# Every second absolute weight sum of the V stage summed on ScalarE instead of VectorE

## The reference

```python
qkv = x @ w_qkv
q, k, v = jnp.split(qkv, 3, axis=-1)            # 16 heads of 64
q = _apply_rope(q, cos, sin); k = _apply_rope(k, cos, sin)
scores = jnp.einsum('bhqd,bhkd->bhqk', q, k) * scale
scores = jnp.where(causal, scores, jnp.finfo(scores.dtype).min)
out = jnp.einsum('bhqk,bhkd->bhqd', jax.nn.softmax(scores, axis=-1), v)
x = _layernorm(x + out @ w_out)

def _weight_quant(w):
    scale = 1.0 / jnp.clip(jnp.mean(jnp.abs(w)), 1e-05)
    return jnp.clip(jnp.round(w * scale), -1.0, 1.0) / scale
def _act_quant(x):
    scale = 127.0 / jnp.clip(jnp.max(jnp.abs(x), axis=-1, keepdims=True), 1e-05)
    return jnp.clip(jnp.round(x * scale), -128.0, 127.0) / scale

gate = silu(bitlinear(x, w_gate)); up = bitlinear(x, w_up)
x = _layernorm(x + bitlinear(gate * up, w_down))
```

## Time and profile before

| | before |
|---|---|
| median of 3 runs | 1207.52 us |
| the profiled execution's own time | 1206.47 us |
| its span, slowest core (core 0) | 1204.9 us |
| spans of the eight cores | 1201.3 to 1204.9 us |
| TensorE busy | 1143.7 us (95%) |
| VectorE busy | 703.1 us (58%) |
| ScalarE busy | 656.2 us (54%) |
| GpSimd busy | 115.3 us (10%) |

### The profile page before, as it was taken

One profiled execution on the slowest core, in us unless ns is written; L12 is line 12 of the kernel. 1 busy time (PEld: TensorE's weight loads), 2 busy tenths in 40 slices (PEclk: granted clock), 3 DMA queues, 4 the chain that ended last, 5 costly groups with the idle time before them and its releaser, 6 DMA issues.

```text
span 1204.9 us, 17116 instructions; the slowest of 8 cores (1201.3 to 1204.9 us)
## 1 busy us (share of the span) xinstructions
PE 1143.7 (95%) x6448; PEld 489.3 (41%) x6470; DVE 703.1 (58%) x999; ACT 656.2 (54%) x815; POOL 115.3 (10%) x185
## 2 busy tenths in 40 slices
PE   3998999999999988999999999999999999999998
PEld 1443333333333322444444444444444444444443
DVE  2359777677678634588874545545544544543343
ACT  3337699998999998354454344344344344342400
POOL 3011134122331230000000000000000000000000
PEclk9999899999999999999999999999999999999999
DMA  9999899976999784567784443443443433332482
GB/s 277 314 323 330 263 310 315 308 243 199 294 320 342 252 291 149 186 168 216 228 206 117 96 115 104 96 122 97 97 122 96 97 96 97 74 102 70 107 161 75
DMA packets 152705, 225.22 MB, mean 187 GB/s; under 512 B 107888, under 2 KB 112112, under 8 KB 137264
## 3 DMA queue, kind: packets, MB, share of 16 engines
q1 hardware_dynamic: 148784, 214.28, 60.7%
q0 software_dynamic: 3840, 9.84, 2.9%
HBM read 148.19 MB, written 46.53 MB: 162 GB/s over the span
## 4 chain that ended last, share of the span: by engine, by line
PE 75%; ACT 10%; DMA 8%; DVE 2%; POOL 2%; issue 1%; POOLq 0%; SPq 0%; DVEq 0%; ACTq 0%
PE sc L868 37%; PE av L932 16%; ACT E L644 7%; PE pj L401 6%; PE pj L787 5%; PE sc L631 4%; DMA ring<-wg 4%; PE av L671 3%; PE su L671 3%; PE sc L932 2%; DMA ring<-xu 2%; POOL swp L74 1%; DMA ring<-wu 1%; ACT Rb L693 1%; DMA swp<-QK 1%; DVE part L497 1%
## 5 line engine op out<-in xcount | busy, mean ns | idle before, releaser
L644 ACT ACTIVATE E<-sc,cst 128x1024 bf16<-128x1024 f32 (+1 forms) x288 | 292.2, 1069 | 32.5 <-PE sc L631 31.6
L878 ACT ACTIVATE sg<-sc,st 128x512 bf16<-128x512 f32 x128 | 87.7, 685 | 305.9 <-PE sc L868 280.5
L868 PE MATMUL sc<-TU,xqT 128*128 128x512 fp8e4 x1024 | 242.0, 379 | 0.0
L868 PE MATMUL sc<-TG,xqT 128*128 128x512 fp8e4 x1024 | 242.0, 379 | 0.0
L932 PE MATMUL av<-TD,hqT 128*128 128x512 fp8e4 x896 | 195.7, 379 | 0.0
L884 DVE TENSOR_TENSOR h<-sc,sg 128x512 f32<-128x512 f32 x128 | 88.2, 689 | 160.2 <-PE sc L868 137.9
L401 PE MATMUL pj<-xT,wqk 128*64 128x512 bf16 (+1 forms) x928 | 142.3, 395 | 19.8 <-DVE xT L354 18.8
L868 PEld LDWEIGHTS sc<-TG,xqT 128*128 128x128 bf16 x1024 | 100.2, 98 | 120.8
L868 PEld LDWEIGHTS sc<-TU,xqT 128*128 128x128 bf16 x1024 | 100.2, 98 | 120.9
L932 PEld LDWEIGHTS av<-TD,hqT 128*128 128x128 bf16 x896 | 87.6, 98 | 105.8
L631 PE MATMUL sc<-QK,QK 64*128 64x512 bf16 (+3 forms) x640 | 110.0, 355 | 21.1 <-ACT E L644 15.0
(11 more groups left out here) (88 smaller groups left out, 921.3 us busy)
## 6 DMA issues: line engine op xcount, KB each, us to landing
ring<-wg SPq DMA_DIRECT2D x28, 1024.0 KB, 19.3
ring<-wu SPq DMA_DIRECT2D x28, 1024.0 KB, 11.4
ring<-wd SPq DMA_DIRECT2D x16, 1024.0 KB, 11.0
dstg<-wd SPq DMA_DIRECT2D x16, 1024.0 KB, 7.0
hqs<-hq SPq DMA_DIRECT2D x64, 256.0 KB, 3.2
ring<-wqk SPq DMA_DIRECT2D x8, 1024.0 KB, 12.6
ring<-xu SPq DMA_DIRECT2D x8, 1024.0 KB, 25.1
swp<-QK POOLq DMA_DIRECT2D x64, 128.0 KB, 8.7
```

Of the source, the lines that this page charges most:

```text
L644: t2 = act.do(lambda e: e.activation(Et[:, :, a:z], out[:, :, a:z], AF.Exp, bias=c_(4), scale=0.125), t, *more)
L868: fn = lambda e, kc=kc, dst=dst, W=W: e.matmul(dst, x_[:, kc, :], W[:, n, kc * 512:(kc + 1) * 512], start=(kc == 0), stop=(kc == 7))
L878: a = act.do(lambda e: e.activation(sg[b], G[b], AF.Silu, scale=col(t, 19)), tm, t_hs[t], sg_free[b])
```

## The change

Of the units that fall into the V stage, every second call of `bg_item` asks for ScalarE, if the unit is an absolute sum and its number is below 12. The calls are counted with the weight conversion as number 1, so units 1, 3, 5, 7, 9 and 11 of the gate weight go to ScalarE and 0, 2, 4, 6, 8, 10 and 12 to 14 stay. ScalarE writes the absolute values over the unit in the ring and adds them up into the column of `part`.

```diff
+        t_parta = []
@@ bg_item
-        def bg_item():
+        def bg_item(on_act=False):
...
-                t = dve.do(lambda e: e.tensor_reduce(part[:, m, n:n + 1], ring[i], AXX, ALU.add,
-                                                     apply_absolute_value=True), tk)
-                t_part[m] = t
+                if on_act and n < 16 - NK:
+
+                    t = act.do(lambda e: e.activation(ring[i], ring[i], AF.Abs,
+                                                      accum_out=part[:, m, n:n + 1]), tk)
+                    t_parta.append(t)
+                else:
+                    t = dve.do(lambda e: e.tensor_reduce(part[:, m, n:n + 1], ring[i], AXX, ALU.add,
+                                                         apply_absolute_value=True), tk)
+                    t_part[m] = t
@@ thresholds
-            a = dve.do(lambda e: e.tensor_reduce(tiny[:, m:m + 1], part[:, m, :], AXX, ALU.add), t_part[m])
+            a = dve.do(lambda e: e.tensor_reduce(tiny[:, m:m + 1], part[:, m, :], AXX, ALU.add), t_part[m], *t_parta)
@@ the V stage
+        nbg = 0
...
-                            bg_item()
+                            nbg += 1
+                            bg_item(nbg % 2 == 1)
```

## The result

| | before | after |
|---|---|---|
| median of six runs each, same chip | 1207.36 us | 1217.76 us |
| median of the fast ones (six, four) | 1207.36 us | 1217.41 us |
| ratio of the fast ones, 95% interval | | 1.0081, 1.0067 to 1.0094 |
| profiled execution, its own time | 1206.47 | 1217.39 |
| spans of the eight cores | 1201.3 to 1204.9 | 1210.9 to 1215.8 |

A forecast was written before the change was run, and what follows sets the result against it. TensorE, 95% busy, was taken as the bound, with holes set by the weights' stream. A stall of about 11 us less the two holes gave +3.5: profiled execution 1206.47 to 1210.0, median 1211.0 us, range 1207.2 to 1214.5.

The forecast's parts named there:

- What bounds the kernel: TensorE, 18 to 130 us, core 0: holes of 3.37 and 3.65 us behind VectorE, whose sums wait for the weights' stream.
- The sum on ScalarE: Each moved sum takes 1.91 us on ScalarE, upper bound 3.57, with no table load.
- The stall: Second `pj` group: TensorE waits 11.0 us, 62.95 to 74.0 on core 0, for ScalarE's copy behind unit 3's sum.
- repaid: Unit 3 lands at most 3.4 us earlier, since the swaps come after it; chance 0.08 for faster by over 0.2%.
- Their 28.21 us should stay: The 16 V tiles after the stall keep their 28.21 us on core 0, as ScalarE's sums find their data there.
- No wait for the rope: At the first scores: rope done by 103 on core 0, ahead of the scores at 108.4.
- From the first scores to the second `Lb`: This stretch takes 18.3 us, as on core 4 at full clock before the change.
- So that hole and its slow stretch vanish: Threshold matmul: the 3.65 us hole and 3.3 lost to slow clock go; second to third `Lb` takes 16.3, not 23.24.
- ready at 122.0 as before: Ahead of the threshold matmul, VectorE's sum is ready at 122.0 (119.73 + 2.29), its load fixed by the stream.
- Measuring at the third `Lb` and adding the rest unchanged: A core that reaches the third `Lb` x later ends x later: 3.1 us on core 0, 3.7 on core 4.
- Slower still: Late swaps make the rope set the first scores at 108 to 113; 1211 to 1216 us; chance 0.15.
- No stall: ScalarE's copies pass the waiting sums, or the moved sums are hidden; change 0, 1207.5 us; chance 0.07.

The follow-up runs named there:

- e1_act_work: Kernel before, with ScalarE also doing six absolute sums of the same size at the same places, over data long in memory; 1206.21 us against 1205.76, ratio 1.0003.
- e2_act_wait: Kernel before, with ScalarE copying one column of the unit at the same six places, each waiting for its load; 1212.48 us against 1205.76, ratio 1.0080.
- e6_rope_early: Kernel before, with the first rope ahead of unit 7's sum in VectorE's list, ScalarE unchanged; 1210.79 us against 1210.01, ratio 1.0004.
- e4_thr_step: Changed kernel with the threshold matmul one attention step later on TensorE; 1210.80 us against 1205.76 for the kernel before, ratio 1.0044.

## Why the prediction was wrong, point by point

- **What bounds the kernel:** the two holes behind VectorE were not all; two small ones, 1.16 us at 25.15 and 1.04 at 41.32 on core 0, stand ahead of the stretch that changed and move nothing in the sum.
- **The sum on ScalarE**, 1.91: right, plus about 0.1 for the read of the accumulator. The Trainium skill, ScalarE: Activation LUTs, section Table sets, was cited for there being no table load, and the trace agrees: none stands behind any of the sums. VectorE's busy time fell by 14.5 us and ScalarE's rose by 10.8 on the slowest cores (core 0 before, core 6 after), forecast 13.7 and 11.5 or more.
- **The stall:** right. TensorE starts again at 72.50 on core 0 and 73.06 on core 4, forecast 74.0 and 72.6; `e1_act_work` and `e2_act_wait` show that the wait in line alone makes it. The wait on core 0 was 5.35 and not 11.0, as TensorE came to it 4.2 later than before (67.15 instead of 62.95); the restart, which ScalarE sets, did not move with that. On core 0 unit 3's sum started at 69.87, 1.6 earlier than before, on core 4 at 70.43, 0.4 later; the mean over the cores is 70.5 in both kernels, so the early landing of the rival "repaid" did not come. The two slow groups took 5.6 and 5.8 us, forecast 6.2 and 5.6.
- **"Their 28.21 us should stay":** this step failed in the first measurement, by 2.5 us on core 4 (from 78.83 to 109.12 it took 30.29, forecast 27.8). It held on the three other chips. Not the sums or the banks were at fault, as I had argued there, but the clock, at 0.91 on average. The cause of that clock stays open.
- **No wait for the rope:** right. TensorE reaches the first scores at 109.12 without a wait. VectorE itself waited 8.14 and 2.94 us for the swaps on core 0 and was done with the rope by 99.9, forecast 103.
- **From the first scores to the second `Lb`:** 18.6 instead of 18.3.
- **"So that hole and its slow stretch vanish":** this failed everywhere. VectorE's part did vanish (on core 0 its sum over the columns came at 123.92, the matmul at 131.06), and behind it stood one that the program's order makes: the matmul goes into `pj` right behind a projection group, so it waits 1.74 us for ScalarE's copy. I had subtracted the whole hole instead of asking what is late next, and then the slow clock as well. On core 4 the step took 19.91 instead of 16.3, 3.6 us. That VectorE would be "ready at 122.0 as before" was off too, without a price: the two sums ahead of it did not wait for loads any more but stood behind an attention product that waited 6.13 for ScalarE.
- **Measuring at the third `Lb` and adding the rest unchanged:** right, within 0.3 us on the first chip.

Core 4 adds up: 0.5 at the stall, 0.2 in the slow groups, 2.5 in the V tiles, 0.3 up to the second `Lb` and 3.6 to the third are 7.1, against 147.61 - 140.6 = 7.0. The threshold step accounts for about half of the miss, and with it alone the forecast would have been some 7 us slower than before. On the other chips the changed kernel lost 4.4 to 5.7. There the kernel before reached the third `Lb` at 139.9 and 140.7 and not at 137.8, which is another part of the difference. That these losses come near the forecast 3.5 is luck: the threshold step was as wrong there (18.4 or 19.9 on every core, not 16.3), and a later kernel before hid it.

Of the rivals none came true as written. "Slower still" named a slower clock as an addition, but put the cause at the rope, where TensorE did not wait. "No stall" is refuted by `e2_act_wait`. The rivals about the gain were half right: `e6_rope_early` shows that what is won ahead of the threshold is given back there.

## What to carry to other kernels

Before an operation moves to an idle engine, ask what it waits for and what is queued behind it there. On an in-order engine, one short instruction that waits for a load holds every PSUM copy behind it, and the engine that fills these banks stops (0.20 us of copying with the wait cost 8.75 us of TensorE in `e2_act_wait`); the busy share of the target says nothing of this. And do not subtract a whole wait because its releaser will be early: look for the next releaser at the same instruction, which is often the bank's last reader and fixed by the program's order.

## What the runs showed of the hardware

- A wait of 1.74 us was enough on some cores for the clock behind it to fall to half (1.2 of 2.4 GHz). Seven of eight cores of the changed kernel lost it in the first measurement, three of eight on each of three other chips, with the same wait. After 0.77 us in `e4_thr_step` none of eight did.
- A third ratio shows between the two levels: in the V tiles of the first chip the granted clock averaged 0.91 on core 4, in spells, with TensorE busy throughout; on core 2 it was 0.81 from 85 to 99 us. On three other chips the same tiles took 27.8 us on all eight cores, with a granted clock of 1.00. The Trainium skill, TensorE: Matmul & The Clock Gate, Part 1, describes 13/16 of the clock on a die when three or more of its cores run dense matmuls, for as long as the load lasts. The spells may be that; but they ended while the load went on, and the sixteen tiles at 1.00 on eight busy cores don't agree with it as a rule for every execution.
- One pair of kernels gave 1.0081 in one measurement and 1.0039 to 1.0047 in three others on three chips, with intervals that don't overlap. Below one per cent a ratio from one measurement is not yet that of the kernel.
